# The correlation with its operands exchanged, copied by ACT and turned back by TensorE

## The reference, cut to what matters

```python
x = x + autocorrelation(layernorm(x), ctx, ctx)      # the change is in here
x = x + lora_ffn(layernorm(x))
x = x + grouped_attention(layernorm(x), ctx, ctx)
x = x + moe_ffn(layernorm(x))

# autocorrelation: per batch, head and channel
corr = ifft(fft(q) * conj(fft(k))).real              # 64 lags for each channel
w, idx = top_k(corr, 8); w = softmax(w)              # the 8 best lags of each channel
out = sum_i w_i * v[min(pos + idx_i, 63)]
```

## Time and profile before

| what | value |
|---|---|
| median of 3 runs | 690.85 us |
| profiled execution | 692.62 us, span 690.8 us |
| mean granted clock of TensorE | 0.986 of full |
| PE busy | 660.0 us (96%) |
| DVE busy | 510.7 us (74%) |
| ACT busy | 432.8 us (63%) |
| POOL busy | 378.0 us (55%) |
| chain that ended last | PE 78%, DVE 13% |

### The profile page before, as it was taken

One profiled execution on the slowest core, in us unless ns is written; L12 is line 12 of the kernel. 1 busy time (PEld: TensorE's weight loads), 2 busy tenths in 40 slices (PEclk: granted clock), 3 DMA queues, 4 the chain that ended last, 5 costly groups with the idle time before them and its releaser, 6 DMA issues.

```text
span 690.8 us, 12651 instructions
## 1 busy us (share of the span) xinstructions
PE 660.0 (96%) x3962; PEld 486.5 (70%) x3962; DVE 510.7 (74%) x1140; ACT 432.8 (63%) x794; POOL 378.0 (55%) x465
## 2 busy tenths in 40 slices
PE   8789999999989998999999999999999999999986
PEld 4446666666656576788787887787878878787775
DVE  4789899999967678677677776776777767774444
ACT  4668888888746775675746747558466574664221
POOL 2447999888866515345445354553545544534451
PEclk8799999999999999999999999999999999999999
DMA  8233534353234431112212222123121220211000
GB/s 268 75 129 102 154 105 152 95 186 116 65 106 108 128 113 50 47 50 63 72 31 61 60 61 61 34 57 87 35 61 47 61 75 30 61 28 50 17 16 30
DMA packets 32695, 54.37 MB, mean 79 GB/s; under 512 B 5360, under 2 KB 7152, under 8 KB 32656
## 3 DMA queue, kind: packets, MB, share of 16 engines
q1 hardware_dynamic: 32656, 53.90, 26.2%
HBM read 36.84 MB, written 8.39 MB: 65 GB/s over the span
## 4 chain that ended last, share of the span: by engine, by line
PE 78%; DVE 13%; issue 3%; ACT 2%; POOL 2%; DMA 0%; DVEq 0%; POOLq 0%; SPq 0%; ACTq 0%
PE wide L1294 7%; PE ps_b L1294 7%; PE wide L1296 6%; PE wide L1295 6%; PE ps_b L1296 6%; PE ps_b L1295 6%; PE ps_a L1339 4%; PE ps_b L1489 4%; PE wide L1407 4%; PE bank L1417 4%; PE ps_b L1349 3%; DVE gmax L1117 2%; PE ps_a L1294 2%; PE ps_a L1296 2%; PE ps_a L1295 2%
## 5 line engine op out<-in xcount | busy, mean ns | idle before, releaser
L779 POOL TENSOR_TENSOR va<-mv,small 128x1 f32<-128x1 f32 x80 | 15.4, 193 | 154.9 <-DVE mv L1273 79.2
L744 ACT ACTIVATE stage<-wide 128x512 f32<-128x512 f32 x30 | 16.3, 595 | 83.6 <-PE bank L1590 83.5
L867 POOL TENSOR_TENSOR y_l<-y,y_h 128x512 fp32r<-128x512 f32 x16 | 21.9, 1372 | 72.4 <-ACT y_h L652 72.4
L1141 DVE RECIPROCAL y<-ps_b 128x256 f32<-128x256 f32 x32 | 55.9, 1748 | 0.4 <-PE ps_b L1489 0.4
L675 ACT ACTIVATE probs<-wide 128x1024 f32<-128x1024 f32 x32 | 32.8, 1026 | 35.8 <-PE wide L1543 35.8
L1294 PE MATMUL wide<-up_h,t_h 128*128 128x512 f32 x128 | 52.4, 409 | 1.5 <-DVE t_l L1225 1.5
L1296 PE MATMUL wide<-up_h,t_l 128*128 128x512 f32 x128 | 50.6, 396 | 0.0
L1295 PE MATMUL wide<-up_l,t_h 128*128 128x512 f32 x128 | 50.3, 393 | 0.0
L1294 PE MATMUL ps_b<-down_h,ht_h 128*128 128x512 f32 x120 | 49.5, 413 | 0.4 <-DVE ht_l L1213 0.4
L781 POOL TENSOR_TENSOR rs<-va,small 128x1 f32<-128x1 f32 x80 | 44.6, 558 | 6.3
L1296 PE MATMUL ps_b<-down_h,ht_l 128*128 128x512 f32 x120 | 47.1, 392 | 0.0
(11 more groups left out here) (245 smaller groups left out, 2166.0 us busy)
## 6 DMA issues: line engine op xcount, KB each, us to landing
q_stack<-qt_h SPq DMA_DIRECT2D x128, 64.0 KB, 2.0
ctx_t<-in_ctx SPq DMA_DIRECT2D x16, 256.0 KB, 2.7
x_res<-in_x SPq DMA_DIRECT2D x16, 256.0 KB, 2.9
x_in<-x_rows SPq DMA_DIRECT2D x16, 256.0 KB, 2.7
ctx_t<-in_ctx_turned SPq DMA_DIRECT2D x16, 256.0 KB, 2.9
x_res<-x_rows SPq DMA_DIRECT2D x16, 256.0 KB, 3.0
out<-stage SPq DMA_DIRECT2D x15, 256.0 KB, 3.0
x_in<-in_x SPq DMA_DIRECT2D x8, 256.0 KB, 2.9
```

The lines of the kernel that those rows point to most:

```text
L1141: dve.reciprocal(y[:, :, b, :], part[:, 1]).then_inc(S["den_s"], 1)
```

## The change

The operands of the correlation change places. `icorr` becomes the stationary operand (64 columns) and `prod` moves through in 512 columns, once for each batch. The two results fill bank 4 with lags on the partitions (batch 0 on 0 to 63, batch 1 on 64 to 127) and channels along the row. ACT copies the bank into `corr_rows`, which is the memory of `kept_not` under another shape. After the values' transform, TensorE turns the copy back into bank 4, 128 channels at a time, and the maxima read what they read before. VectorE's `prod` now waits for the first matmuls of the tile before (`corr_raw`) and the maxima for the transposes (`corr_ps`). Two semaphores that nobody waited for are gone.

```diff
+        corr_rows = kept_not[:].rearrange("p c s -> p (c s)")
...
                 layer_out(i - 2)
+                t = i + 2
+                if live(t):
+                    act.wait_ge(S["corr_raw"], t + 1)
+                    wait(act, S["sub_s"], t)
+                    act.activation(corr_rows, bank[4], ACT.Copy).then_inc(S["corr_s"], 1)
...
-                    act.activation(v[:, 0].rearrange("p b n -> p (b n)"), ps_b[:], ACT.Copy).then_inc(S["vf_s"], 1)
+                    act.activation(v[:, 0].rearrange("p b n -> p (b n)"), ps_b[:], ACT.Copy)
...
-                    wait(dve, S["corr_ps"], t)
+                    wait(dve, S["corr_raw"], t)
...
-                    for c in range(DC):
-                        for b in range(2):
-                            k = slice(P * c + SEQ * b, P * c + SEQ * (b + 1))
-                            last = pe.matmul(bank[4][:, k], prod[:, b, P * c:P * (c + 1)], icorr, start=True, stop=True)
-                    last.then_inc(S["corr_ps"], 1)
+                    for b in range(2):
+                        last = pe.matmul(bank[4][SEQ * b:SEQ * (b + 1), :], icorr, prod[:, b, :], start=True, stop=True)
+                    last.then_inc(S["corr_raw"], 1)
...
                     context(ps_b, V0, t).then_inc(S["v_ps"], 1)
+                    pe.wait_ge(S["corr_s"], t + 1)
+                    for c in range(DC):
+                        last = pe.transpose(cols(bank[4], c, P), cols(corr_rows, c, P), ident)
+                    last.then_inc(S["corr_ps"], 1)
```

More of the change, by code:

```diff
@@ L252, in build @@
             stage_hi stage_lo
-            dft_hi dft_lo c1_hi c1_lo nm1_s nb1_s nm2_s nb2_s x_loaded x_odd_loaded ctx_loaded res_loaded bn1_s mv1_s va1_s rs1_s xn1_s
-            q_ps qf_s k_ps prod_s v_ps vf_s vsw_s corr_ps tops_s shift_s exp_s rep_s sum_s inv_s sub_s wgt_s
+            dft_hi c1_hi c1_lo nm1_s nb1_s nm2_s nb2_s x_loaded x_odd_loaded ctx_loaded res_loaded bn1_s mv1_s va1_s rs1_s xn1_s
+            q_ps qf_s k_ps prod_s v_ps vsw_s corr_raw corr_s corr_ps tops_s shift_s exp_s rep_s sum_s inv_s sub_s wgt_s
             wt_ps wt_s wf_ps prod2_s o_ps x1_s bn2_s mv2_s va2_s rs2_s xn2_s
@@ L1014, in _ @@
             dve.wait_ge(S["dft_hi"], 1)
-            dve.tensor_tensor(dft_l[:], dft[:, K0:W0], dft_h[:].bitcast(F32), ALU.subtract).then_inc(S["dft_lo"], 1)
+            dve.tensor_tensor(dft_l[:], dft[:, K0:W0], dft_h[:].bitcast(F32), ALU.subtract)
             first_context(0)
```

## The result

| | before | changed |
|---|---|---|
| median | 691.03 us (4 runs, 690.18 to 691.28) | 714.20 us (4 runs, 712.26 to 714.39) |
| ratio | | 1.0331, 95% interval 1.0311 to 1.0351 |
| profiled execution, span | 692.62, 690.8 | 714.36, 712.5 |
| PE busy | 660.0 us (96%) | 663.5 us (93%) |

The change costs 23 us. In the changed kernel the exponential (L628) has 40.3 us of idle time before its 16 runs, all ended by the small subtraction L1087; in the kernel before (L622, L1081) it was 3.0 us. Columns: busy, mean ns of one, idle before and what ended it; the kernel before comes first.

What follows compares the result with a forecast made beforehand. TensorE bounded pass 1, VectorE second; the change would hold VectorE's small subtraction behind GpSimd's split. 7.2 (narrow) + 8.6 (wide) + 1.6 (start) + 0.9 (end) = 18.3 us on the 690.85 median gives 709.1; range 692 to 715.

Steps and rivals of the forecast that it cites:

- TensorE's work: TensorE, each pass 1 turn: correlation 1.93 out, matmuls 0.94 and transposes 0.44 in; work falls 0.55 to 10.68 us.
- The maxima, M = C + 2.76: VectorE's eight maxima start (M) 2.76 us after the correlation starts (C), 0.19 later than before, once transposes are done.
- The lead: GpSimd's split of a staged weight (C + 4.41) starts 0.11 us before VectorE's small subtraction (C + 4.52).
- An unheld turn gives nothing (11.21): Pass 1 turn without collision: 2.76 + 2.01 + 6.44 = 11.21 us, so TensorE's saving is lost in the keys' wait.
- The 6.44 behind the exponential: From the exponential's start over ACT's normalisation, swapped copies, keys' transform and output group to the next correlation: 6.44 us.
- The collision: VectorE's small subtraction held behind GpSimd's split: narrow-piece turns 12.26 us, wide 13.38; 7 narrow turns cost 7.2.
- Wide turns: Turns with staged pieces 1024 wide: held, each 2.15 us longer; four cost 8.6, the first of five passes.
- Rival 4: The forecast, plus the granted clock falling as TensorE idles: five falls at 1.5 us each, 717; chance 0.09.
- Start 1.6: First three turns: late copy and half-clock transposes +0.9, then 0.4 and 0.3; sum 1.6 us, bounds -1 and +3.
- end 0.9: Last weights of pass 1: copied by ACT at 197.1 instead of 196.18, +0.9 us.
- Rival 1: Small subtraction still first, or not held by so small a lead; turns stay 11.21, 693 us; chance 0.18.
- Rival 3: Not slower: TensorE's 10.68 sets the pace if maxima to next correlation is below 8.2; 684 to 688; chance 0.06.

Runs made afterwards that it cites:

- e10_swapped_small_add: e5_after_swapped with GpSimd's second add of the FFN's result cut from 512 to 8 columns; 699.34 us, ratio 1.0121.
- e8_one_maximum: The kernel before with one extra maximum, its result unread, ahead of VectorE's eight; 707.00 us, ratio 1.0210.
- e5_after_swapped: The changed kernel with VectorE's two subtractions in the other order, the small one of two SBUF operands first; 706.10 us, ratio 1.0190.
- e2_two_maxima: The kernel before with two extra maxima, their results unread, ahead of VectorE's eight; 705.75 us, ratio 1.0214.
- e6_two_swapped: The kernel before with two extra maxima ahead of the eight and VectorE's two subtractions in the other order; 693.29 us, ratio 1.0031.
- e4_turned_early: The changed kernel with TensorE's four transposes ahead of the values' transform and ScalarE's copy earlier in its queue; 693.31 us, ratio 1.0026.
- e3_exchange_alone: The changed kernel without ScalarE's copy and TensorE's four transposes, so the maxima read wrong values; 687.20 us, ratio 0.9915.

## Why the prediction was right

709.1 was forecast for 714.2, inside the range and by the mechanism named. Step by step:

- **TensorE's work.** Correlation 0.86, not 0.94. Transposes 0.60, not 0.44, and the turning of the weights now took 0.59 in the chain (before 0.44). Most of that difference is one of reading. The chain counts a group from the modelled end of the one before; counted from start to start in the timeline the turning took 0.54 before (130.20 to 130.74) and 0.59 now (131.52 to 132.11). Work fell by about 0.3 and, as said, was worth nothing.
- **The maxima, M = C + 2.76.** Wrong by 0.2: C + 2.98 = 0.86 + 0.59 + 0.91 + 0.60 + 0.02. The two groups of four transposes, taken at 0.44 each from the chain, were the mis-sized terms. ACT's copy was covered: it ended 0.5 ahead of the transposes in turn 7 and 0.08 ahead in turn 2. (By the forecast's own rows, C + 1.70 + 0.60, it would have been 0.02 late.)
- **The lead.** 0.11 was forecast, 0.36 measured (135.50 - 135.14): the error of M was twice the margin on which the forecast stood. It fell on the safe side, as the forecast had argued that errors would, but that the margin wasn't lost to it is in part luck. The size didn't matter, since in a held turn POOL's start sets the end, and that start was right to the hundredth (135.14 - 130.73 = 4.41).
- **An unheld turn gives nothing (11.21).** It costs: 11.46 in turn 1 and in e10_swapped_small_add. The 6.44 behind the exponential was exact (142.99 - 136.55); the 0.25 are 0.20 of M, 0.04 from M to the exponential (the eight maxima took 1.15 for 1.12) and 0.01 behind it.
- **The collision.** Forecast 12.26 and 13.38, measured 12.26 and 13.36. Narrow turns 7.2, measured 7.2. The first wide turn passed, as taken, and for the reason given (the split 0.34 later after C, +4.92 for +4.58); but with M 0.2 late it was a tie, not a lead of 0.2. The Trainium skill's page "SBUF — State Buffer", section "SBUF: two separate sides", was followed where it says that whoever starts first holds the ports throughout. The runs agree: a lead of 0.05 cost as much as one of 0.36, in e8_one_maximum as in the changed kernel the held subtraction ended 0.08 after the split, and a held low half of 512 columns ended 0.54 to 0.55 after POOL's add, whether that add took 0.21 (e10_swapped_small_add) or 1.27 (e5_after_swapped). That the bank-reading subtraction isn't held also agrees with that section's restriction to two SBUF inputs (0.68 to 0.69 in every run).
- **Wide turns.** 8.6 forecast, 9.4 measured: 1.15 of it is the one fall of the clock in turn 2, less 0.3 since turn 5 of before was itself 0.3 long (11.52). Rival 4 had priced five falls at 1.5 each; one came, at 1.15.
- **Start 1.6, measured 3.0; end 0.9, measured 2.1.** The waits named are there, but these 5 us can't be put down to them. At the start the copy ran until 16.80 and the transposes took 1.1 at half clock, and the first turn took 15.74 for 13.19. But kernels with the start of before, but for the extra maxima (e2_two_maxima, e8_one_maximum, e6_two_swapped) reached the third correlation at 38.6, 40.0 and 39.9, before at 38.5; kernels with the changed start reached it at 38.5 (e10_swapped_small_add) to 40.8 (the changed kernel). Both cover the same range. The granted clock doesn't set the two apart either: from 12 to 24 its mean was 0.72 in both kernels. At the end ACT's copy of the last weights began at C + 13.03 (217.13 - 204.10), before at C + 11.65: 1.4 later, for 0.9 forecast; behind it 218 to 222 ran at 0.50 (before 0.66 in 198 to 202). But from the correlation of turn 13 to the end of the span the kernel before took 506.3, e2_two_maxima with the same end 504.3 and the changed kernel 508.4, so a scatter of 2 us is as large as what was to be explained. What start and end cost stays open.
- **Rivals.** Rival 1 (693) needed VectorE ahead of the split, that is the subtraction about 0.35 earlier than it came (0.1 earlier than forecast); e4_turned_early, where it stands 0.10 ahead of the split, took 693.31. Rival 3 (TensorE sets the pace) fell: e3_exchange_alone took 11.03 a turn with TensorE's own work near 10.2 (11.23 - 1.93 + 0.86), and the path behind M was as forecast. The limit of 8.2 that the rival named doesn't follow from its terms, though: with 10.68 and M at C + 2.76 it would be 7.92.

The prediction did not see that removing the hold would uncover the next pair, and that waits put in against a hold cost as much as it did.

## What to carry to other kernels

Before moving work on one engine, list the VectorE instructions with two SBUF operands and the GpSimd instructions that start within some tenths of a us of them: a delay of 0.13 us can flip their order and cost nearly the length of the GpSimd instruction in every turn of a loop (1.0 of 1.3 us, 2.15 of 2.4). The cheap remedy is to reorder within VectorE's own queue, so that the two-operand instruction starts well ahead, and then to look where it lands in the turns whose GpSimd work starts earlier; both waits that were tried on GpSimd moved its whole queue. Before relieving the busiest engine, read what the next wait stands on: 0.9 us less for TensorE was worth 0.2.

## What the runs showed that was not expected

- The tie is decided within hundredths. In e10_swapped_small_add the small add on POOL and the low half on VectorE meet in turns 6 to 11, POOL recorded 0.02 to 0.03 ahead each time. In two of the six POOL was held (0.77 for 0.21) and VectorE was not, in the other four VectorE was held (0.72 for 0.68); at such a lead the record doesn't tell which (VectorE, then POOL, two turns):

```profile
127.91 0.68 DVE L1017 TENSOR_TENSOR c_l<-ctx_t,c_h 128x512 fp32r<-128x512 f32 x1
...
139.38 0.72 DVE L1017 TENSOR_TENSOR x_l<-ctx_t,x_h 128x512 fp32r<-128x512 f32 x1
```

```profile
127.89 0.77 POOL L809 TENSOR_TENSOR x_odd<-x_odd,b_all 128x8 f32<-128x8 f32 x1
...
139.35 0.21 POOL L809 TENSOR_TENSOR x<-x,b_all 128x8 f32<-128x8 f32 x1
```

- The same group of four 128-column transposes took 0.44 in the chain of the kernel before and 0.59 to 0.60 in the changed one, but 0.54 and 0.59 from start to start. The 0.05 that is left goes with what stands ahead: the turning of the weights took 0.54 in e8_one_maximum, with the old correlation ahead of it, and 0.59 in e3_exchange_alone, with the new one. The cause wasn't tried.
- Beside the experiments the kernel before spread over 687.9 to 694.7 us, its executions below 690.5 at a mean granted clock of 0.990 to 0.994, the others at 0.982 to 0.989; a few us between two single executions say nothing here.
